# Scan stage of a hybrid block: the drives of six of sixteen states are made in token-major form on ScalarE and transposed into PSUM by TensorE

## What is computed

```python
xz = einsum('bld,ed->ble', x, W_in)              # 128 -> 2 * 256 channels
u, z = split(xz, 2)
u = silu(causal_conv1d(u, conv_w, conv_b))       # 4 taps
dt, Bm, Cm = split(einsum('bld,rd->blr', u, W_x), [8, 8 + 16])
dt = softplus(dt @ W_dt.T + b_dt)                # one step size per channel
dA  = exp(dt[..., None] * A)                     # decay, 16 states per channel
dBu = dt[..., None] * Bm[:, :, None, :] * u[..., None]   # drive
h = dA_t * h + dBu_t                             # over the 1024 tokens
y = einsum('bdn,bn->bd', h, C_t) + u * D
y = y * silu(z);  out = y @ W_out.T
```

## Time and profile before

| | before |
|---|---|
| time, median of 3 runs | 2417.92 us (2416.85 to 2421.42) |
| time of the profiled execution | 2413.16 us |
| its span, first to last instruction | 2411.4 us |
| busy in the span: TensorE / VectorE / ScalarE / GpSimd | 87% / 69% / 43% / 61% |
| scans of the Mamba block (L1685) | 416 + 96, from 937.8 us on |
| mean granted TensorE clock, share of full | 0.941 |

### The profile page before, as it was taken

One profiled execution on the slowest core, in us unless ns is written; L12 is line 12 of the kernel. 1 busy time (PEld: TensorE's weight loads), 2 busy tenths in 40 slices (PEclk: granted clock), 3 DMA queues, 4 the chain that ended last, 5 costly groups with the idle time before them and its releaser, 6 DMA issues. The chain is left out here.

```text
span 2411.4 us, 43664 instructions
## 1 busy us (share of the span) xinstructions
PE 2087.2 (87%) x15450; PEld 1540.6 (64%) x15451; DVE 1661.8 (69%) x2661; ACT 1036.6 (43%) x1967; POOL 1479.8 (61%) x871
## 2 busy tenths in 40 slices
PE   5888789999999986877788787887768999999998
PEld 3656554499999942444555444554555449999994
DVE  6888848333333365999999999999993843333335
ACT  4444432222222225777666666666623222222222
POOL 3555500167666603999998989889880017667660
PEclk9888889999999997999999999989878999999999
DMA  7000010000000123233232322332206000000014
GB/s 272 1 0 0 1 36 0 5 26 25 24 25 24 24 74 123 93 108 102 84 102 85 101 86 86 93 106 90 96 35 234 0 4 26 24 25 25 24 24 109
DMA packets 65005, 146.01 MB, mean 61 GB/s; under 512 B 8923, under 2 KB 42717, under 8 KB 54406
## 3 DMA queue, kind: packets, MB, share of 16 engines
q1 hardware_dynamic: 55814, 126.06, 15.8%
q0 software_dynamic: 9088, 18.63, 2.8%
HBM read 128.01 MB, written 16.65 MB: 60 GB/s over the span
## 5 line engine op out<-in xcount | busy, mean ns | idle before, releaser
L1634 POOL TENSOR_TENSOR m_seen<-m_state,experts 128x1024 f32<-128x1024 f32 x256 | 600.9, 2360 | 85.5 <-DVE m_state L1685 80.9
L979 PE MATMUL f_up_ps<-f_xT,f_weights 128*128 128x128 f32 x3976 | 488.5, 277 | 10.9 <-issue 8.2
L1685 DVE TENSOR_TENSOR_SCAN m_state<-experts,m_ps 128x512 f32<-128x512 f32 x416 | 495.9, 1233 | 0.0
L979 PEld LDWEIGHTS f_up_ps<-f_xT,f_weights 128*128 128x128 f32 x3976 | 469.9, 193 | 16.3 <-issue 15.9
L1091 POOL DMA_INDIRECT f_xin<-tokens,f_take x142 | 141.1, 994 | 374.9 <-DVE f_take L764 263.8
L803 DVE TENSOR_TENSOR f_hT<-f_gated,f_up_ps 128x512 f32<-128x512 f32 x142 | 97.7, 688 | 326.8 <-ACT f_gated L885 326.8
L1360 PEld LDWEIGHTS m_ps<-ident,m_seen 128*128 128x128 f32 x2048 | 253.3, 150 | 106.5 <-issue 54.9
L1360 PE MATMUL m_ps<-ident,m_seen 128*128 128x128 f32 x2048 | 290.7, 290 | 18.9 <-POOL m_seen L1634 18.9
L1019 PE MATMUL f_y_ps<-experts,f_hT 128*128 x2272 | 277.1, 275 | 0.9 <-DVE f_yout L816 0.9
L1516 ACT ACTIVATE experts<-m_delta,experts 128x512 f32<-128x512 f32 x416 | 267.2, 710 | 4.1 <-DVE m_state L1685 3.8
L1349 PE MATMUL m_ps<-m_parts,m_spread 96*128 96x512 bf16 x416 | 138.0, 416 | 150.4 <-DVE m_state L1685 149.1
(11 more groups left out here) (228 smaller groups left out, 3170.6 us busy)
## 6 DMA issues: line engine op xcount, KB each, us to landing
experts<-m_rows SPq DMA_DIRECT2D x64, 1024.0 KB, 4.7
experts<-in_experts SPq DMA_DIRECT2D x17, 1461.0 KB, 19.3
experts<-m_rows SPq DMA_DIRECT2D x16, 768.0 KB, 8.1
tokens<-f_rows SPq DMA_DIRECT2D x8, 512.0 KB, 5.5
f_rows<-expert_out SPq DMA_DIRECT2D x8, 512.0 KB, 7.3
f_cols<-expert_out SPq DMA_DIRECT2D x8, 512.0 KB, 7.2
f_xin<-tokens,f_take POOLq DMA_INDIRECT x142, 2.6
expert_out<-f_yout,f_back_to POOLq DMA_INDIRECT x142, 2.2
```

Of the source, the lines that this page charges most:

```text
L979: mm = pe.matmul(up_ps[:, bank + k, col:col + P], weights[:, s, at:at + P], xT[:, s, :], start=True, stop=True)
L1634: pool.tensor_tensor(seen[:, n % SEEN], state[:, n % RING], c_rep[:, Q % C_RING, n % C_GROUP, :].unsqueeze(1).to_broadcast([P, HALF, SEG]) ...
L1685: dve.tensor_tensor_scan(state[:, n % RING, h, :], decay_, drive_, before_, ALU.mult, ALU.add).then_inc(s_state, 1)
```

## The change

Six states per unit, `ACROSS` = 2, 5, 7, 10, 13, 15, get their drive in another way. Once per unit TensorE transposes B (`turn_b`, at step 12) and delta_u (`turn_delta_u`, at step 14) to token-major form, and ScalarE copies both out of PSUM (`columns_b`, `delta_u_across`). In that form B of one state is one number per partition, so ScalarE makes the drive as four activations 128x256 with a per-partition scale (`scale`). TensorE turns it back with eight transposes straight into `PB` (`upright`), in place of `rows_b` and of VectorE's `drive`.

With it: `AWAY` is cut from three states to two (4, 12), so state 8 becomes an ordinary one with `rows_b` and `drive`. The C rows come in groups of 2 with a ring of 4 (before: groups of 4, ring of 3). The convolution's bias is no longer a pass of its own (one half at step 2, one at step 4): at step 4 Silu reads both halves out of PSUM with the bias, and Silu of z is an instruction of its own after it. `DECAYED`, the table of when each decay is made, differs in two entries.

```diff
-                RING, DECAYS, B_RING, SEEN, C_GROUP, C_RING = 4, 8, 2, 4, 4, 3
-                AWAY = (4, 8, 12)
-                AWAY_AT = {15: 4, 3: 8, 6: 12}
+                RING, DECAYS, B_RING, SEEN, C_GROUP, C_RING, SCALED = 4, 8, 2, 4, 2, 4, 2
+                AWAY = (4, 12)
+                AWAY_AT = {15: 4, 6: 12}
+                ACROSS = (2, 5, 7, 10, 13, 15)
+                ACROSS_AT = {15: 2, 1: 5, 3: 7, 8: 10, 10: 13, 13: 15}
...
-                DECAYED = [[2, 3], [5], [6], [4], [], [7, 9], [10], [8], [11], [], [13], [12, 14], [15], [], [NS], [NS + 1]]
+                DECAYED = [[2, 3], [5], [6], [4], [], [7, 8], [9], [10], [11], [], [13], [12, 14], [15], [], [NS], [NS + 1]]
...
+                        def turn_b(V):
+                            pe.wait_ge(s_bc, V + 1)
+                            pe.wait_ge(s_read0, nth0["b", V])
+                            for i in range(TILES):
+                                mm = pe.transpose(SIDE0[:, i * NS:(i + 1) * NS], bc[0:NS, i * P:(i + 1) * P], ident[0:NS, 0:NS])
+                            mm.then_inc(s_side0, 1)
+
+                        def turn_delta_u(V):
+                            pe.wait_ge(s_dtu, V + 1)
+                            pe.wait_ge(s_read0, nth0["du", V])
+                            pe.wait_ge(s_read1, nth1["du", V])
+                            for k, s_side in enumerate((s_side0, s_side1)):
+                                for i in range(k * 2, k * 2 + 2):
+                                    for h in range(HALF):
+                                        at = i % 2 * DI + h * P
+                                        mm = pe.transpose(SIDES[:, k, at:at + P], delta_u[:, V % 2, h, i * P:(i + 1) * P], ident[:])
+                                mm.then_inc(s_side, 1)
+
+                        def upright(G):
+                            U, n = divmod(G, NS)
+                            pe.wait_ge(s_scaled, nth_across[G] + 1)
+                            pe.wait_ge(s_state, (G - B_RING + 1) * HALF)
+                            for h in range(HALF):
+                                for i in range(TILES):
+                                    mm = pe.transpose(PB[:, n % B_RING, h, i * P:(i + 1) * P], scaled[:, nth_across[G] % SCALED, i, h * P:(h + 1) * P], ident[:])
+                            mm.then_inc(s_upright, 1)
...
+                        turn_b(0)
+                        turn_delta_u(0)
                         pe.wait_ge(s_set, NL * HALF)
...
                             if G + 1 in nth_drive:
                                 rows_b(G + 1)
+                            if G + 1 in nth_across:
+                                upright(G + 1)
...
-                        def convolved(V, h):
...
-                            act.activation(u(V)[:, h, :], bank, ACT.Identity, bias=conv_b[:, lh:lh + 1]).then_inc(s_read, 1)
-
                         def silu(V):
-                            act.wait_ge(s_read0, nth0["conv", V] + 1)
-                            act.wait_ge(s_read1, nth1["conv", V] + 1)
-                            both = zu[:, V % 2] if V else u(V)
-                            act.activation(both, both, ACT.Silu).then_inc(s_silu, 1)
+                            l = UNITS[V][0]
+                            for h, (s_side, s_read, nth) in enumerate(((s_side0, s_read0, nth0), (s_side1, s_read1, nth1))):
+                                act.wait_ge(s_side, nth["conv", V] + 1)
+                                act.activation(u(V)[:, h, :], SIDES[:, h, :], ACT.Silu, bias=conv_b[:, l * HALF + h:l * HALF + h + 1]).then_inc(s_read, 1)
+                            if V:
+                                silu_gate(V - 1)
                             act.preload_act_table_set("natural_log_exp_and_others")
...
+                        def delta_u_across(V):
+                            wait(act, s_scaled, len(ACROSS) * V)
+                            for k, (s_side, s_read, nth) in enumerate(((s_side0, s_read0, nth0), (s_side1, s_read1, nth1))):
+                                act.wait_ge(s_side, nth["du", V] + 1)
+                                act.activation(across[:, k * 2:k * 2 + 2, :].rearrange("p i d -> p (i d)"), SIDES[:, k, :], ACT.Copy).then_inc(s_read, 1)
+
+                        def scale(G):
+                            U, n = divmod(G, NS)
+                            k = nth_across[G]
...
+                            wait(act, s_upright, k - SCALED + 1)
+                            for i in range(TILES):
+                                ins = act.activation(scaled[:, k % SCALED, i, :], across[:, i, :], ACT.Copy, scale=b_across[:, i * NS + n:i * NS + n + 1])
+                            ins.then_inc(s_scaled, 1)
...
+                            if n in ACROSS_AT:
+                                m = ACROSS_AT[n] + (NS if ACROSS_AT[n] < n else 0)
+                                if U * NS + m < STEPS:
+                                    scale(U * NS + m)
```

More of the change, by code:

```diff
@@ L1180, in mamba @@
                 decay = lodge(NL * HALF * NS)
+                across = lodge(TILES * DI).rearrange("p (i d) -> p i d", d=DI)
+                b_across = lodge(TILES * NS)
+                scaled = lodge(SCALED * TILES * DI).rearrange("p (r i d) -> p r i d", r=SCALED, d=DI)
                 rows_out = [nc.dram_tensor(f"m_rows_{k}", (2 * NS, SEG), F32, kind="Internal").ap() for k in range(2)]
@@ L1203, in mamba @@
                 s_turned, s_back, s_y = ts("turned"), ts("back"), ts("y")
+                s_scaled, s_upright = ts("scaled"), ts("upright")
                 first_weights = [(in_wT, "m_inT"), (conv_b[:], "m_conv_b"), (skip[:], "m_skip"), (decay, "m_A_log")]
@@ L1227, in columns_in @@
                     return (xT if l == 0 else hT)[:, s, at:at + SEG]
[L1229 to L1230 removed]
+                CONV0, CONV1, Y_COPY, BACK, SILU, OUT, ROWS, DT, SOFT, SKIP, DELTA, DELTA_U, GATE, B_TURN, TURN, DU_TURN = (0, 1), (2, 3), 2, 4, 4, 5, 6, (7, 8), 9, (9, 10), 9, 11, (11, 12), 12, 13, 14
+                DECAYED = [[2, 3], [5], [6], [4], [], [7, 8], [9], [10], [11], [], [13], [12, 14], [15], [], [NS], [NS + 1]]
                 ADDED = [[-2], [-1], [], [0], [1], [2], [3], [4], [5], [6], [7], [8], [9], [10, 11], [12], [13]]
[L1233 to L1234 removed]
+                uses0 = [("turn", 0), ("conv", 0), ("turn", 1), ("gate", 0), ("b", 0), ("du", 0)]
+                uses1 = [("conv", 0), ("gate", 0), ("du", 0)]
                 for U in range(N_UNITS):
@@ L1242, in mamba @@
                     if V < N_UNITS:
-                        uses0 += [("dt0", V), ("dt1", V), ("gate", V)]
+                        uses0 += [("dt0", V), ("dt1", V), ("gate", V), ("b", V), ("du", V)]
                         uses1.append(("gate", V))
@@ L1251, in mamba @@
                 nth_decay = {G: k for k, G in enumerate(decayed)}
-                driven = [G for G in range(STEPS) if G % NS not in AWAY]
+                driven = [G for G in range(STEPS) if G % NS not in AWAY + ACROSS]
+                nth_across = {G: k for k, G in enumerate(G for G in range(STEPS) if G % NS in ACROSS)}
                 nth_drive = {G: k for k, G in enumerate(driven)}
@@ L1276, in _ @@
                             wait(sp, s_away, len(AWAY) * V)
-                            sp.dma_start(b_rep, rows_out[V % 2][AWAY[0]:NS:AWAY[0], :].unsqueeze(0).to_broadcast([P, len(AWAY), SEG])).then_inc(s_b_rep, 16)
+                            sp.dma_start(b_rep, rows_out[V % 2][AWAY[0]:NS:AWAY[1] - AWAY[0], :].unsqueeze(0).to_broadcast([P, len(AWAY), SEG])).then_inc(s_b_rep, 16)
                             for g in range(GROUPS):
@@ L1440, in _ @@
                                     gate(V, n - GATE[0])
+                                if n == B_TURN:
+                                    turn_b(V)
                             if n == TURN and U + 2 < TURNS:
                                 turn(U + 2)
+                            if n == DU_TURN and V < N_UNITS:
+                                turn_delta_u(V)
                             if n in SKIP:
@@ L1480, in round_high @@
                             act.activation(bc[0:XR], SIDE1[0:XR], ACT.Copy).then_inc(s_bc, 1)
-                            wait(act, s_b, (V - 1) * (NS - len(AWAY)))
+                            wait(act, s_b, (V - 1) * (NS - len(AWAY) - len(ACROSS)))
                             act.activation(parts[0:32, V % 2, :], SIDE1[0:32], ACT.Copy).then_inc(s_rounded, 1)
@@ L1547, in _ @@
                         act.activation(decay[:], decay[:], ACT.Exp).then_inc(s_exp_A, 1)
-                        for h in range(HALF):
-                            convolved(0, h)
                         silu(0)
@@ L1566, in _ @@
                             gated(0, h)
+                        columns_b(0)
+                        delta_u_across(0)
+                        scale(ACROSS[0])
                         for G in range(STEPS):
```

41 lines of the change are left out of this document (27 added, 14 removed).

## The result

The changed kernel takes 2452.47 us (median of 4 runs, 2441.19 to 2455.13), the kernel before 2417.39 (4 runs). The ratio is 1.0136, 95% interval 1.0100 to 1.0172: slower by 1.4%, where 2379 had been forecast, and above the upper end of the range, 2424.

The account below looks back on a forecast made before the run. VectorE was taken as the bound: 47.7 us busy plus 4.2 waiting make a unit 51.9 instead of 54.29. Gains of 36 and 5.6 less 3 turn 2413.16 into 2374.6, as a median 2379; range 2330 to 2424.

Parts of the forecast that it names:

- (a): Step 4: VectorE's `gate_y` waits 2.3 us for `turn_back`, which must follow ScalarE's decay, copies of state 7, table load and Silus.
- (b): Steps 1 to 2: TensorE has 3.7 us of work in a 2.24 us step, so `drive(3)` waits 0.9 us for row 3.
- (c): Step 10: ScalarE's copies of state 10 follow the row projection and rounding; `upright(10)` starts 1.3 us late, row 11 at most 1.3.
- (d): End of the unit: row 0 of the next unit is late by up to 1.4 us up to unit 5, later by 0.5.
- today's waits: VectorE's 0.96 us a unit for the spread B row before the change; not added, since TensorE "will idle less".
- I take 4.2: VectorE's waits per unit taken as 4.2 us, where (a) to (d) add to 5.9 in units 0 to 5 and 5.0 after.
- the start: Before step 0 TensorE waits for ScalarE's copies and turns B and delta_u before spreading row 1: a loss of 3 us.
- Of the rivals, the second: The drives only turn into waits: six uprights each 0.7 us late, or (a) to (d) at 6.6; 2411 to 2421, 8%.
- Its other reading: Each of the six `upright` is late by 0.7 us, which brings the unit back to 54.3 us.
- The third, a clock kept low by transposes: TensorE's clock stays low from step 12 to step 1, VectorE waits 9 us more a unit; 2514 us, 8%.
- The fourth, ScalarE's sum: ScalarE becomes the bound: at 0.62 us a scaled copy the unit is 54.3 us, at 0.68 the kernel 2440; 10%.

Follow-up runs that it names:

- the old Silu: The changed kernel with the Silu part undone: bias passes at steps 2 and 4, then one Silu over 2048 columns; 2410.76 us, ratio 0.9970.
- the two fastest runs: Changed kernel with scaled copies of state 7 at step 4, state 10 at step 5: 2382.54 us; the same with `accumulate` ahead of `turn_back` at step 4: 2379.05 us.
- the run with both moves and the old Silu: Changed kernel with scaled copies of state 7 at step 4 and of state 10 at step 5, and the Silu part undone; 2393.08 us, ratio 0.9886.
- the sums ahead of `turn_back`: Changed kernel with scaled copies of states 7 and 10 at steps 4 and 5, and TensorE's `accumulate` transposes before `turn_back` at step 4; 2379.05 us, ratio 0.9829.

## Why the prediction was wrong

Point by point, per unit, forecast and measured:

| | forecast | measured |
|---|---|---|
| VectorE busy | 47.7 | 48.2 |
| GpSimd busy | 47.0 | 47.0 |
| TensorE busy | 48.0 | 47.6 |
| ScalarE busy | 46.1 | 45.8 |
| (a) `gate_y`, step 4 | 2.3 | 2.7 |
| (b) step 2 | 0.9 | 0.87 |
| (c) step 10 | 1.3 | 3.7 |
| (d) row 0, step 15 | 0.5 to 1.4 | 0.34 |
| step 13 | 0 | 0.48 |
| step 7 | 0 | 0.72 |
| all waits | 4.2 | 8.85 |
| unit | 51.9 | 57.03 |

The work was priced right, the copies too: 384 of them are busy 162.8 us, 0.424 each, for the 0.42 taken. The kind of loss was right as well: four of the six waits stand where the text put them. What failed is their size, in three steps of it.

The first and largest is (c), 1.3 forecast and 3.7 measured, and in it "From there it has six decays' halves, four copies of the step sizes, two roundings and then the scaled copies of state 10: 7.1 us". By the text's own prices these pieces add to 8.6 us (6 x 0.62, 4 x 0.5, 2 x 0.59 and 1.65), and in the unit with full clock they take 9.0, with four roundings and four halves of decays; VectorE then waits 1.76 us. The rest, 1.9 us a unit, goes with TensorE's clock. The text took the links of (a) to (d) at full clock, although the clock of the stage was 0.92 before, and put what is left of today's waits at nothing because TensorE "will idle less". It did idle less, 9.5 us a unit for 11, but the clock stayed at 0.92, and now its low stretches lie on a chain that VectorE waits for: in the unit shown a step projection took 2.07 us for 1.12, `upright(10)` 1.97 for 1.09. The runs confirm the place: making the copies of state 10 earlier takes 51 us off, making them twice adds 26.

The second is "I take 4.2", for places that the text itself had added up to 5.0 to 5.9, on the ground that a VectorE that waited in step 4 finds the others ahead later. It doesn't: at full clock the wait in step 10 is 1.76 us behind a `gate_y` that waited 3.3, and the same with the old Silu, where `gate_y` waits 0.2.

The third are steps 7 and 13, put at nothing, with 1.2 us. In step 7 VectorE waits for the row of state 8, an ordinary state now, and TensorE spreads that row only behind the row projection of step 6. In step 13 it waits for the row of state 14, which TensorE spreads behind `upright(13)`, a gate matmul, `turn_b` and eight transposes, from 1217.82 to 1220.96 in the unit shown.

The sum around it: the start was costed at 3 us and shows 3.8 in the second drive. Of the 4 us or so that the text's terms give for the eleven steps behind the fifteenth `gate_y`, 2.5 came. The text expected the median 4.8 us above the profiled execution, and it is 2.7 below, which is little beside a miss of 73.

Of the rivals, the second came nearest ("or (a) to (d) came to 6.6"): they came to 7.6, and with steps 7 and 13 to 8.8, past no change and into slower. Its other reading, six uprights each a little late, is not what the trace has: scans waited 22 us in all 14 units, drives 64. The third, a clock kept low by transposes, is refuted as written: the clock of the stage was 0.92 as before, and 0.98 and 0.99 in the two fastest runs with the same transposes. The Trainium skill's rule ("TensorE: Matmul & The Clock Gate", "Part 4: PE-mode transpose"), by which transposes don't engage the full clock, is not borne out by these runs. But a low clock is a good part of the loss all the same, by its falls in steps 7 to 12. The fourth, ScalarE's sum, is refuted by the two runs with copies made twice, and the run with both moves and the old Silu doesn't bring it back.

What stays open: what brings the clock down in steps 7 to 12 where TensorE had hardly idled, as at 1201.4; how much of the 51 us of the early copies is the shorter chain and how much the clock that then stays up; and what the 4 us of waiting a unit in the fastest versions would need.

The change's idea carries: with its six copies at other steps it is 1.6% faster than the kernel before, and within 4 us of what had been forecast for the change as it was.

## What to carry to other kernels

When all engines run fixed lists, a saving on the bound engine is worth only what the chains past it allow, and these are priced link by link: each link's own work, what it waits for on the other engine, and that engine's clock while it waits. Add the waits of one iteration up as they are: here no wait covered another. And compare single iterations of one run by their granted clock before you call a low clock a mere consequence: here units with the same work differed by 4 us. Before judging a change that moves work to another engine, try its places: here two numbers in a table of places, with the same instructions on every engine, made 2452 us into 2383.

## What the runs showed of the hardware

An activation 128x256 with a per-partition scale took 0.495 us and came every 0.42 us. An estimate from the Trainium skill's formula for an activation with one pointer operand ("ScalarE: Activation LUTs", "What ACT_TABLE_LOAD costs") gives about 0.49, and the trace agrees. Transposes kept TensorE at 2.4 GHz: with the sums ahead of `turn_back`, the granted clock was 0.99 over 728 us in which some 2,700 of its 3,745 matmul instructions were transposes. It went to 1.2 GHz at some of the waits, such as the 2.36 us before `turn_back`, and not at others: in the unit with full clock TensorE waited 2.18 us before `upright(10)` and stayed at 2.4 GHz. It also went to 1.2 GHz at about 1201.4, where TensorE had idled 0.47 us in ten.
